# Attention stage of a two-layer kernel: queries and keys turned by transposing transfers, scores in four banks, next tile's projections ahead of the scores

## What is computed

```python
DIM, HEADS, B, T, CHUNK = 512, 16, 4, 512, 128
q, k, v = split(x @ w_qkv.T)                       # 32 columns a head
q = concat([q * cos(th), q * sin(th)])             # 64 columns a head; k the same
# per head and chunk of 128 tokens:
scores = (q_i @ k_i.T) * diag_decay                # 128 x 128, causal
o      = scores @ v_i + (q_i * q_decay) @ state
state  = block_decay * state + (k_i * k_decay).T @ v_i
y      = o @ w_proj.T
```

## Time and profile before

| | |
|---|---|
| median of the runs | 1573.32 us |
| the profiled execution | 1575.18 us |
| its span, first to last instruction | 1573.2 us |
| TensorE busy in the span | 1429.3 us, 91% |
| VectorE, ScalarE, GpSimd busy | 952.3, 694.5, 772.0 us |
| mean granted TensorE clock | 0.959 |
| first attention | 0 to 316 us |

### The profile page before, as it was taken

One profiled execution on the slowest core, in us unless ns is written; L12 is line 12 of the kernel. 1 busy time (PEld: TensorE's weight loads), 2 busy tenths in 40 slices (PEclk: granted clock), 3 DMA queues, 4 the chain that ended last, 5 costly groups with the idle time before them and its releaser, 6 DMA issues.

```text
span 1573.2 us, 32803 instructions
## 1 busy us (share of the span) xinstructions
PE 1429.3 (91%) x10839; PEld 800.5 (51%) x10840; DVE 952.3 (61%) x1858; ACT 694.5 (44%) x1282; POOL 772.0 (49%) x691
## 2 busy tenths in 40 slices
PE   5999999899999999999997359999999999999990
PEld 2555665544444444445444225666666666666650
DVE  7877777776767666635988874444444444444435
ACT  6533333455454545434344523444444444444443
POOL 3565544620010102044545536777676777777655
PEclk9999999999999999999999569999999999999995
DMA  6334221369796979553204545888888888776766
GB/s 243 115 100 121 47 47 40 99 223 324 237 296 230 282 243 291 169 164 81 83 3 100 184 136 119 176 169 185 186 184 193 195 186 205 138 113 94 174 80 228
DMA packets 149453, 254.96 MB, mean 162 GB/s; under 512 B 67945, under 2 KB 69513, under 8 KB 148368
## 3 DMA queue, kind: packets, MB, share of 16 engines
q1 hardware_dynamic: 113776, 194.62, 38.8%
q0 software_dynamic: 35616, 59.58, 23.5%
HBM read 158.92 MB, written 101.71 MB: 166 GB/s over the span
## 4 chain that ended last, share of the span: by engine, by line
PE 69%; DVE 16%; issue 6%; POOL 4%; ACT 3%; DMA 2%; SPq 0%; DVEq 0%; POOLq 0%; ACTq 0%
PE bank L904 20%; PE bank L925 11%; PE bank L590 8%; PE bank L731 6%; PE bank L737 6%; PE bank L754 6%; PE bank L895 5%; PE bank L914 2%; POOL ARENA L1688 1%; DVE ARENA L1276 1%; POOL ARENA L1693 1%; DVE ARENA L1042 1%; ACT ARENA L1405 1%; DVE ARENA L995 1%; DVE bs L971 1%
## 5 line engine op out<-in xcount | busy, mean ns | idle before, releaser
L904 PE MATMUL bank<-ARENA,XT 128*128 x1908 | 364.7, 327 | 2.9 <-issue 2.7
L1824 POOL DMA_INDIRECT accs<-X,WA x159 | 252.5, 1588 | 94.1 <-issue 39.7
L904 PEld LDWEIGHTS bank<-ARENA,XT 128*128 128x128 f16 x1908 | 180.4, 98 | 126.5 <-issue 10.5
L1366 DVE COPY XT<-bank 128x1024 f16<-128x1024 f16 x159 | 109.9, 691 | 181.2 <-PE bank L895 145.2
L1817 POOL DMA_INDIRECT XT<-x_rows,WA x159 | 166.5, 1047 | 93.7 <-issue 41.2
L925 PE MATMUL bank<-ARENA,XT 128*128 x795 | 197.4, 379 | 0.8 <-issue 0.7
L1405 ACT ACTIVATE ARENA<-ARENA 128x512 f16<-128x512 f32 (+2 forms) x128 | 89.2, 708 | 245.9 <-DVE ARENA L1124 131.6
L1647 ACT ACTIVATE XT<-bank 128x192 f32<-128x192 f32 x159 | 52.5, 330 | 286.3 <-PE bank L904 235.7
L590 PE MATMUL bank<-XT,STG 128*128 128x512 f16 x640 | 151.2, 384 | 7.4 <-DVE ARENA L1170 7.3
L1675 POOL TENSOR_TENSOR rstd<-mv,mhalf 128x1 f32<-128x1 f32 x28 | 8.7, 309 | 250.4 <-DVE mv L974 250.4
L590 PE MATMUL bank<-WA,XT 128*128 128x512 f16 (+1 forms) x732 | 127.1, 327 | 2.9 <-DVE ARENA L1023 2.1
(11 more groups left out here) (245 smaller groups left out, 2347.5 us busy)
## 6 DMA issues: line engine op xcount, KB each, us to landing
w_scratch<-WA SPq DMA_DIRECT2D x64, 640.0 KB, 3.9
ARENA<-w_scratch SPq DMA_DIRECT2D x64, 640.0 KB
ARENA<-w_exp SPq DMA_DIRECT2D x48, 640.0 KB, 5.2
WA<-w_exp SPq DMA_DIRECT2D x16, 640.0 KB, 5.1
ARENA<-ARENA SPq DMA_DIRECT2D x64, 128.0 KB, 2.3
accs<-ARENA SPq DMA_DIRECT2D x20, 256.0 KB, 3.4
X<-x SPq DMA_DIRECT2D x4, 1024.0 KB, 5.8
ARENA<-wc SPq DMA_DIRECT2D x8, 512.0 KB, 6.0
```

Of the source, the lines that this page charges most:

```text
L904: mm = pe.matmul(d, xTb[k.u % 2][:, a * KD + kd, :], weights(sl, b, kd * 2 * DFF, 2 * DFF), start=(a, b, kd) == (0, 0, 0), stop=(a, b, kd) ...
L1366: dve.tensor_copy(xTb[k.u % 2].rearrange("p c n -> p (c n)"), bank[k.u % 2][:, :].bitcast(F16)).then_inc(xt_sb, 1)
L1824: pool.indirect_dma_start(accs, bass.IndirectOffsetOnAxis(blkout[:, i:i + 1], 0), yD[i % 8], None, compute_op=ALU.add).then_inc(y_out[i % ...
```

## The change

- `transposed` and both `evacuate` go. SP's `turn(n)` takes their place and that of `swap`: wait for `q_split` and for the reads of `QA` by tile n-2 (`qa_free`), one transposing transfer `QT` to `QA` (128x2048 float16), wait until it has landed, two transfers `QA` to `QB` (64 partitions x 16 heads each), wait for `k_split`, one transposing transfer `KTk` to `KA`.
- `scores` has four banks (4, 5, 3, 7) and waits for no decay; all its waits stand ahead of group 0.
- TensorE's order becomes `out_proj(t-1)`, `to_state(t)`, query and key projections of t+1, `scores` 0 to 3, `from_state(t)`, half of the value projection of t+1 (now in bank 2), `from_chunk(t)`, its other half.
- VectorE rotates the next tile's queries and keys ahead of the decays; `stateL` moves to the tile's end, the decay of the state to its start.
- ScalarE makes `q_high(t+1)` ahead of `stateH` and `k_high(t+1)` behind it; both wait also for the transfer that reads their buffer. GpSimd makes the decayed keys between `q_low` and `k_low`.

```diff
-            def swap(t):
-                for h0, ready in ((0, evac_act), (8, evac_dve)):
-                    sp.wait_ge(ready, t * 2 + 1)
-                    for p in (0, 64):
-                        sp.dma_start(QB[p:p + 64, h0:h0 + 8, :], QA[64 - p:128 - p, h0:h0 + 8, :]).then_inc(swapped, 16)
+            def turn(count):
+                sp.wait_ge(consts_in, 16 * 2)
+                sp.wait_ge(q_split, count)
+                sp.wait_ge(qa_free, count)
+                sp.dma_start_transpose(QA, QT.rearrange("p h n -> p (h n)")).then_inc(q_moved, 16)
+                sp.wait_ge(q_moved, count * 16)
+                for p in (0, 64):
+                    sp.dma_start(QB[p:p + 64, :, :], QA[64 - p:128 - p, :, :]).then_inc(swapped, 16)
+                sp.wait_ge(consts_in, 16 * 2)
+                sp.wait_ge(k_split, count)
+                sp.dma_start_transpose(KA, KTk.rearrange("p h n -> p (h n)")).then_inc(k_moved, 16)
...
             def scores(t, g):
                 if g == 0:
-                    pe.wait_ge(evac_act, t * 2 + 2)
-                    pe.wait_ge(swapped, t * 64 + 64)
+                    pe.wait_ge(state_lo, t + 1)
                     pe.wait_ge(r_ready, t)
-                if g == 2:
-                    pe.wait_ge(evac_dve, t * 2 + 2)
-                if g >= 2:
-                    pe.wait_ge(s_decayed, t * 4 + g - 1)
+                    pe.wait_ge(swapped, t * 32 + 32)
+                    pe.wait_ge(k_moved, t * 16 + 16)
                 for h in range(4 * g, 4 * g + 4):
-                    d = bank[4 + g % 2][:, (h % 4) * P:(h % 4 + 1) * P]
+                    d = sbank[g][:, (h % 4) * P:(h % 4 + 1) * P]
...
             def attention(t, first, last):
-                transposed(t, 0)
-                transposed(t, 1)
                 if not first:
                     out_proj(t - 1)
-                transposed(t, 2)
-                transposed(t, 3)
                 to_state(t)
-                scores(t, 0)
-                pe.wait_ge(state_lo, t + 1)
-                pe.wait_ge(o_ready, t)
-                pe.wait_ge(evac_dve, t * 2 + 1)
-                scores(t, 1)
+                if not last:
+                    proj(t + 1, 0).then_inc(q_ready, 1)
+                    pe.wait_ge(state_ready, t + 1)
+                    proj(t + 1, 1).then_inc(k_ready, 1)
+                for g in range(4):
+                    scores(t, g)
                 from_state(t)
-                scores(t, 2)
-                scores(t, 3)
                 if not last:
-                    proj(t + 1, 0, bank[0], q_ready)
-                    pe.wait_ge(state_ready, t + 1)
-                    proj(t + 1, 1, bank[1], k_ready)
+                    proj(t + 1, 2, 0, 6)
                 from_chunk(t)
                 if not last:
-                    pe.wait_ge(q_mul, t + 2)
-                    proj(t + 1, 2, bank[0], v_proj)
+                    proj(t + 1, 2, 6).then_inc(v_proj, 1)
...
@@ VectorE, attention(t)
-                decay(t, 0)
                 dve.wait_ge(kv_ready, t + 1)
                 dve.scalar_tensor_tensor(st, bank[1][:, 0:PAIRS * HD], kp, st, ALU.mult, ALU.add).then_inc(state_ready, 1)
...
                 if not last:
                     rotate(t + 1, 0)
...
+                    rotate(t + 1, 1)
+                for g in range(4):
+                    decay(t, g)
+                dve.wait_ge(qa_free, t + 2)
+                own.did(dve.tensor_tensor(ot, bank[6][:, :], qdec.rearrange("p a b -> p (a b)"), ALU.mult))
+                if isinstance(t, int) and t == 1:
+                    angles(3)
...
                 dve.tensor_tensor(oL, oT, oH, ALU.subtract).then_inc(o_lo, 1)
+                dve.wait_ge(state_hi, t + 1)
+                dve.tensor_tensor(stateL, state, stateH, ALU.subtract).then_inc(state_lo, 1)
```

More of the change, by code:

```diff
@@ L416, in _ @@
             xt_move(1, 0, hlA, None)
-            swap(2)
+            turn(3)
             load_piece(13)
@@ L420, in _ @@
             xt_move(2, 1, hlA, 16 * 1)
-            swap(3)
+            turn(4)
             load_piece(14)
@@ L435, in _ @@
             sp.dma_start(s_upT, ins["s_up"]).then_inc(b_small, 16)
-            with sp.Fori(7, NT) as t:
-                xt_move(t - 1, t - 2, hlA, None)
-                swap(t)
+            with sp.Fori(8, NT + 1) as n:
+                xt_move(n - 2, n - 3, hlA, None)
+                turn(n)
             def prep_load(n, s):
@@ L592, in three, with proj @@
                 return mm
-            def proj(t, j, dst, done):
+            def proj(t, j, lo=0, hi=3 * KD):
                 tk = bass.ds(t * P, P)
-                three(dst[:, :], lambda a, k: XT[:, a, k, tk], lambda b, k: Wqkv[:, b, k, j * DIM:(j + 1) * DIM]).then_inc(done, 1)
+                for n in range(lo, hi):
+                    (a, b), k = ((0, 0), (0, 1), (1, 0))[n // KD], n % KD
+                    mm = pe.matmul(bank[j][:, :], XT[:, a, k, tk], Wqkv[:, b, k, j * DIM:(j + 1) * DIM],
+                                   start=n == 0, stop=n == 3 * KD - 1)
+                return mm
             def first_proj(j, dst, done):
@@ L1057, in attention @@
             def attention(t, first, last):
-                evacuate(t, 1)
+                kp = keep[:, bass.ds(t, 1)]
+                own.did(dve.scalar_tensor_tensor(state, state, kp, decS.unsqueeze(2).to_broadcast([P, PAIRS, HD]), ALU.mult, ALU.mult))
+                own.settle()
                 if first:
@@ L1464, in attention @@
                 v_copy(t)
-                evacuate(t, 0)
-                if last:
-                    convert(0)
-                evacuate(t, 2)
                 if first:
@@ L1473, in attention @@
                 if last:
-                    convert(1)
-                act.wait_ge(state_ready, t + 1)
-                act.wait_ge(inter_ready, t + 1)
-                copy(stateH, state).then_inc(state_hi, 1)
+                    convert(0)
                 if not first:
@@ L1481, in attention @@
                     copy(hlA[:, 0, :], tile(t - 1)).then_inc(x_hi, 1)
+                if last:
+                    convert(1)
+                else:
+                    q_high(t + 1)
                 if isinstance(t, int) and LATE + t < NPA:
                     hi_piece(LATE + t)
+                act.wait_ge(state_ready, t + 1)
+                act.wait_ge(qa_free, t + 2)
+                copy(stateH, state).then_inc(state_hi, 1)
+                if last:
+                    convert(2)
+                else:
+                    k_high(t + 1)
                 if first:
```

89 lines of the change are left out of this document (27 added, 62 removed).

## The result

The changed kernel takes 1560.15 us, the median of four runs (1556.97 to 1564.03), against 1572.74 of the kernel before (four runs now, 1571.47 to 1575.03): a ratio of 0.991, interval 0.989 to 0.993. It is faster by 0.9%, but 12.6 us were gained where 30.7 were forecast, and 1560.15 lies above the range of 1533 to 1557. The profiled execution of it took 1556.97 us, its fastest. I compare it with that of before, 1575.18, which was slower than all four runs; so the two profiles show 18.2 us where the medians show 12.6. Of these 18.2 the first attention, the only stage that was changed, gave 15.3: the feed-forward part starts at 300.84 instead of 316.16 us. The rest of the program, behind that start, is the same in every kernel here, and yet took from 1251.9 to 1259.7 us in the twelve profiles.

The account below looks back on a forecast made before the run. TensorE was taken to bound the kernel: steady tiles of 15.55 us plus unsteady first and last tiles put feed-forward at 285.4 instead of 316.16, 30.7 us earlier; 1575.18 became 1544.5, less 1.9 for the median 1542.6, range 1533 to 1557.

Parts of the forecast that it names:

- `q_split` for the next turn comes at about F+14.9. No queueing: SP's queue: `turn` moves past `xt_move`, which has issued by F+12.9, before `q_split` releases the turn; no delay counted.
- the 0.7 us for the loads: Int8 weights and other loads ahead of a turn: may hold one back by 1 to 3 us; 0.7 us counted.
- the new wait at the output projection: TensorE at `out_proj`, steady tile: waits for the output sum's high half, copied by ScalarE at F+4.0; 0.4 us.
- the lower of the two bounds: Queries' 128x2048 transposing transfer: 4.3 us if start and tail are paid once, 6.1 if all doubles; 4.4 taken.
- The half-guess about line 1096: VectorE's subtraction for the output's low half: taken as 1.0 us, the row without `k_low` beside it, not 2.20.
- Rival C: Line 1096's subtraction keeps running into GpSimd: TensorE waits 0.5 us on 14 tiles, time 1549.6; chance 0.12.
- The step that puts `angles(3)` between the two halves of the output sum: Tile 1, VectorE: 4.06 and 0.43 us that nothing covers; `out_proj(1)` starts at F+7.8 instead of F+4.0.
- the lower clock in the first and the last tile alone: TensorE: cold part of tile 0 at twice the steady row; 2 us counted for products behind the last tile's wait.
- the keys' transfer: Issued 1.2 us into the swaps, data queued behind theirs: 6.65 us, landing at F+11.25 against a cover of 12.8.
- B: The transfers decide: the doubled one costs 6.1 us, 0.8 us a tile on 14 tiles, 2.4 in the last; 1556; chance 0.17.
- D: Slower than before: a 128x2048 transfer costs over two 128x1024 ones; gain gone from 6.8 us, 1594 at 7.5; chance 0.06.
- The rule on transposes weighed there: Skill's rule: 128x128 transposes on TensorE where PSUM will do as destination, otherwise transfers; by it the change is a loss.

Follow-up runs that it names:

- the second run: The changed kernel profiled and timed again with no edit, as base for three edited kernels on its chip: 1561.67 us, ratio 0.992 to the kernel before.

## Why the prediction was wrong

Its mechanism was right, and so was its steady tile; the sum failed in the tiles that are not steady. Three steps failed: "`q_split` for the next turn comes at about F+14.9. No queueing", the 0.7 us for the loads, and the second and the last tile, where slow products behind a wait were left out and a wait was taken too short. Counted in F, the end of the state reads:

| | forecast | measured | off by |
|---|---|---|---|
| F(0) | 39.8 | 39.9 | 0.1 |
| tile 0 to 1 | 18.0 | 18.7 | 0.7 |
| tile 1 to 2 | 19.4 | 22.5 | 3.1 |
| tiles 2 to 6 | 62.2 | 66.3 | 4.1 |
| tile 6 to 7 | 16.25 | 20.9 | 4.6 |
| tiles 7 to 14 | 108.9 | 109.6 | 0.7 |
| F(14) to feed-forward | 20.8 | 23.1 | 2.3 |

Together 15.5 us but for rounding, on a feed-forward forecast at 285.4 and found at 300.84. The time is off by 17.5. The 2 us between come from outside the stage: the median lies 3.2 us above the profiled execution, where the forecast had taken it 1.9 below, and against that the rest of the program was 2.8 us shorter than in the profile of before.

- **Right, the steady tile.** 15.65 for 15.55; the new wait at the output projection 0.2 to 0.3 for 0.4; no decay waited for; the queries' transfer 4.27 us for 4.4, near the lower of the two bounds. The half-guess about line 1096 (1.0 us, though the earlier trace rows had 2.20) was on the right side: 0.69. `k_low` ended 0.2 us ahead of it, as reckoned (F+3.8 and F+4.0), so narrow a margin that it also took luck. Rival C fell in the steady tile, but came true in one tile of the change as made (5 to 6, 2.69 us), and its mechanism is shown by two kernels (2.41 and 2.26 us). The Trainium skill's page SBUF — State Buffer, section "SBUF: two separate sides", describes this exclusion; the rows here agree to 0.15 us: GpSimd's instruction has 119.86 - 117.99 = 1.87 us to go when the subtraction starts, and with 0.69 behind it that is 2.56 for the 2.41 measured; for the kernel with the decays first it is 2.40 for 2.26.
- **Right in kind, too small: the second tile.** The step that puts `angles(3)` between the two halves of the output sum took its 4.06 us from the earlier trace rows. There one GpSimd instruction stood beside it (line 1704, from 58.48 to 60.79); here it took 6.11, beside three. That the GpSimd instructions made it longer is read from this overlap, no kernel tests it. It made `out_proj(1)` start at F+8.85 instead of F+7.8; the larger part of the miss was 2.0 us of slow products behind the idle time. The forecast reckoned with the lower clock in the first and the last tile alone, though a wait of 4 us is a wait of 4 us wherever it stands. The 0.7 us of tile 0 to 1 are not explained.
- **Overlooked: GpSimd's queue in tiles 2 to 5.** The forecast gave the queries' transfer a start of F+0.1 in every tile. It named what `turn` is moved past on SP, but not what stands ahead of `q_low` on the engine that releases it. `split_piece` (line 1704 then) stood there before as well, and cost nothing: it ended at 81.49, and GpSimd then waited 1.13 us more for the queries' high half. The new order makes that high half earlier, and so leaves the split as what `q_low` waits for. Of the 4.1 us it is 2.4, by the kernel with the split ahead of `x_low`; 0.4 are the steady tile's 0.1, 0.9 are waits for transfers that stay, and 0.4 are not explained.
- **Mis-sized: the weights load.** 0.7 us was counted where it measured 5.2 and, again, 7.5. The text had said "may hold back one turn by 1 to 3 us", then took less than the lower end of that. What it missed is that the turn starts only when `xt_move` has issued behind the load (4.68 us for 1.23): the queries' transfer came 3.0 us late and took 1.6 us longer. Less the 1.0 us of cover that is the wait of 3.65, and 1.4 us of slow scores stand behind it. In the second run a transfer of the `instruction` queue lies on the same path.
- **Mis-sized: the keys' transfer.** Forecast 6.65 us behind the swaps' issue, which is 5.45 behind its own; measured 6.4 in the steady tiles of the kernel with the doubled swap, and 7.6 in the last. The steady tile absorbed it (cover 1.0 for 1.5). The last one did not: 5.46 us of wait for the 3.6 forecast, 1.9 of the 2.3 us in the last line of the table. Of the 7.6, 1.3 go with the transfer of the `instruction` queue, by the kernels that do without; the forecast had no such term. The two converts on the path behind it were in the forecast; that 3.2 us could be had back by issuing them earlier was not.
- **The rivals.** B named the transfers as what decides, at 1556, and is nearest to the time by number, but by luck: line 637 waits in no steady tile, and the transfer did not cost 6.1 us. Where transfers do hold a tile, they were issued late or stood behind a load. D did not come near: 4.27 us against its threshold of 6.8. The rule on transposes weighed there (the Trainium skill, VectorE: DVE Perf Modes, "Rules for kernel authors") would have made the change a loss; the steady tile is 2.1 us shorter. No kernel here undid the transposing transfers alone, so how these 2.1 us divide between them and the order is open, but for the four banks (1.41) and the keys' rotation (0.56), each of which is what is lost without it.

The chances were sound on the sign (0.93 for faster). The range was too narrow because its width came from the steady tile, times fourteen, while seven tiles are not steady.

## What to carry to other kernels

When a stage loses its slack, price each of its unsteady tiles by its own trace: what was hidden there for as long as the bounding engine was slower is now late, and it can be late by more than its length, since TensorE ran at its lower clock behind waits of 3.15 us and more here (behind one of 1.49 us it did not). For each wait that a change adds, walk back to the engine that ends it and read what stands in its queue ahead of the release, tile by tile. Bulk loads that nobody waits for belong between the transfers that are waited for, one to a tile.

## What the runs showed of the hardware

- A transposing transfer of 128x2048 float16 within SBUF holds SP's queue for 1.8 us in a steady tile when nothing else is under way and for 4.2 us behind two swaps of 256 KB each. Whatever SP should issue next comes that much later.
- Long idle time costs twice. After 4.97 us of it, twelve products took 4.75 us instead of 2.76; after 3.15 us, in every tile of the kernel with the doubled swap, 32 took 3.4 instead of 1.9.
- A transfer of the `instruction` queue, 0.02 MB, goes with 1.3 us more for a transposing transfer that is under way: in the last tile the keys are there 7.6 to 7.7 us after their issue in the eight profiles that have it, and 6.3 in the three that don't. Which engine it serves, and what moves it from run to run and edit to edit, is open.
